# Inverse roots from one activation table, and the order of work around the first self-attention

## The reference, cut to what matters

```python
x = x + tanh(g_xattn) * xattn(layernorm(x), ctx)        # 16 heads of 128, 361 context tokens
h = layernorm(x)                                        # (x - m) / sqrt(v + 1e-5)
a = rms(h, w_ln1)                                       # x * rsqrt(mean(x^2) + 1e-6) * w
q, k, v = a @ wq + bq, a @ wk + bk, a @ wv + bv         # 16 heads of 32
q, k = rope(q, k)
h = h + softmax(causal(q @ k.T * 32**-0.5)) @ v @ wo
b = rms(h, w_ln2)
route = top_2(softmax(b @ w_router))                    # 8 experts
out = x + tanh(g_ffn) * (h + routed(b) + silu(b @ g) * (b @ u) @ d * sigmoid(b @ eg))
```

## Time and profile before

| | |
|---|---|
| median of 3 runs | 1021.59 us |
| lowest, highest run | 1018.97 us, 1024.71 us |
| the profiled execution's own time | 1021.96 us |
| its span, first to last instruction | 1020.2 us |
| mean granted clock of PE | 0.956 of full speed |
| busy: PE, DVE, ACT, POOL | 900.8, 659.8, 588.1, 391.8 us |
| table loads on ACT | 27, of 1283 ns each |

### The profile page before, as it was taken

The page is one execution under the profiler, slowest core; times in us unless marked ns, Lnnn a source line. Parts: engine busy times, 40 slices in busy tenths (PEclk is TensorE's granted clock), DMA queues, the critical chain, the costliest instruction groups (busy, mean ns, idle before and its releaser), DMA issues.

```text
span 1020.2 us, 16174 instructions
## 1 busy us (share of the span) xinstructions
PE 900.8 (88%) x5713; PEld 829.2 (81%) x5713; DVE 659.8 (65%) x1504; ACT 588.1 (58%) x1455; POOL 391.8 (38%) x367
## 2 busy tenths in 40 slices
PE   5999999999999999989775888898985898988896
PEld 4889999999989999989644866787984887877785
DVE  3557777734657777747565765674655778786653
ACT  3656766644556666634488325675443667776751
POOL 3432222346522222347211732342045365565531
PEclk9999999999999999999775998899998899999998
DMA  5762000045500000054111221132267699999875
GB/s 142 210 227 76 1 1 1 11 128 147 162 27 16 1 1 2 12 146 128 32 46 31 74 70 52 52 94 78 88 221 204 199 301 278 305 280 289 273 189 142
DMA packets 125689, 120.76 MB, mean 118 GB/s; under 512 B 12645, under 2 KB 96557, under 8 KB 125009
## 3 DMA queue, kind: packets, MB, share of 16 engines
q1 hardware_dynamic: 106510, 96.09, 30.8%
q0 software_dynamic: 5120, 10.22, 4.9%
q10 hardware_dynamic: 13978, 13.41, 4.6%
HBM read 102.16 MB, written 17.53 MB: 117 GB/s over the span
## 4 chain that ended last, share of the span: by engine, by line
PE 50%; DMA 17%; DVE 12%; ACT 10%; issue 5%; POOL 4%; SPq 0%; ACTq 0%; POOLq 0%; DVEq 0%
PE bank L1968 45%; DMA eraw<-in_L_ffn_w_down_e_dram 5%; DMA eraw<-in_L_ffn_w_up_e_dram 4%; PE bank L2095 3%; DMA s_sum<-yo,target 3%; ACT PF L1087 2%; DVE we L1313 2%; ACT we L878 2%; POOL s_rows L1901 1%; DMA s_rows<-HR,idx 1%; ACT wf L864 1%; DMA sums<-s_sum 1%; POOL wx L1832 1%; DMA raw<-in_L_xattn_Wo_dram 1%; ACT L1087 1%
## 5 line engine op out<-in xcount | busy, mean ns | idle before, releaser
L1861 POOL TENSOR_SCALAR SC<-SC,mx,anyv 100x361 f32<-100x361 f32 x128 | 81.5, 647 | 211.0 <-DVE mx L1426 200.8
L1844 POOL TENSOR_TENSOR we<-eraw,we 128x704 fp32r<-128x704 f32 x40 | 70.7, 1768 | 138.1 <-ACT we L878 137.8
L878 ACT ACTIVATE we<-eraw 128x704 fp32r<-128x704 f32 (+2 forms) x140 | 97.0, 719 | 45.9 <-DMA eraw<-in_L_ffn_w_up_e_dram 20.9
L1313 DVE TENSOR_TENSOR we<-eraw,we 128x704 fp32r<-128x704 f32 (+2 forms) x100 | 94.1, 956 | 44.9 <-ACT we L878 44.8
L1832 POOL TENSOR_TENSOR wx<-raw,wx 128x512 fp32r<-128x512 f32 x64 | 84.0, 1320 | 93.6 <-ACT wx L864 93.5
L1832 POOL TENSOR_TENSOR wf<-raw,wf 128x512 fp32r<-128x512 f32 x48 | 63.6, 1328 | 137.2 <-ACT wf L864 137.2
L1968 PE MATMUL bank<-H2h,wf 128*128 128x400 f32 x352 | 105.2, 363 | 9.4 <-DVE wf L1313 6.6
L993 ACT ACTIVATE SC<-SC,mx 100x361 f32<-100x361 f32 x128 | 75.4, 593 | 27.8 <-DVE mx L1422 27.2
L1968 PEld LDWEIGHTS bank<-H2h,wf 128*128 128x128 f32 x352 | 68.5, 197 | 12.7 <-DVE wf L1313 8.4
L1968 PE MATMUL bank<-XTh,wx 128*128 128x400 f32 x256 | 72.6, 357 | 3.2 <-POOL wx L1832 1.9
L1968 PE MATMUL bank<-QOh,wx 128*128 128x400 f32 x256 | 73.8, 357 | 0.0
(11 more groups left out here) (266 smaller groups left out, 2787.1 us busy)
## 6 DMA issues: line engine op xcount, KB each, us to landing
eraw<-in_L_ffn_w_gate_e_dram SPq DMA_DIRECT2D x40, 352.0 KB, 4.1
eraw<-in_L_ffn_w_up_e_dram SPq DMA_DIRECT2D x40, 352.0 KB, 5.4
eraw<-in_L_ffn_w_down_e_dram SPq DMA_DIRECT2D x40, 256.0 KB, 6.1
raw<-in_L_xattn_Wq_dram SPq DMA_DIRECT2D x32, 256.0 KB, 3.1
raw<-in_L_xattn_Wo_dram SPq DMA_DIRECT2D x32, 256.0 KB, 3.0
raw<-in_L_ffn_w_sh_gate_dram SPq DMA_DIRECT2D x22, 256.0 KB, 2.9
raw<-in_L_ffn_w_sh_up_dram SPq DMA_DIRECT2D x22, 256.0 KB, 3.4
s_rows<-Z SPq DMA_DIRECT2D x6, 800.0 KB
```

The costliest lines, as they stand in the source:

```text
L878: eng.activation(weights("e", u)[0:rows, 0, 0:n], eraw[u % 6][0:rows, 0:n], ACT.Copy).then_inc(sem("act_e"), 1)
L1313: return eng.tensor_tensor(o, src, f32(hi), ALU.subtract)
L1844: eng.tensor_tensor(w[0:rows, 1, 0:n], eraw[u % 6][0:rows, 0:n], f32(w[0:rows, 0, 0:n]), ALU.subtract).then_inc(sem("pool_e"), 1)
L1861: eng.tensor_scalar(sc, sc, m[:, 3, h:h + 1], anyv[:, b:b + 1], ALU.mult, ALU.mult).then_inc(sem("pool_p"), 1)
```

## The change

Each inverse root becomes two activations, exp(-0.5 * ln(var + eps)), in a helper `inverse_root`, and the reciprocals on DVE go away. Ln and Exp are both in the table `natural_log_exp_and_others`, which is loaded by hand in three places: as ACT's first instruction, after the Tanh of the two gates, and ahead of the last four roots. The compiler still adds loads for Tanh and Silu. In all 7 loads are left of 27.

The order changes too. All eight `qk(1, n)` now stand beside steps 12 to 19 of the first self-attention (five stood beside steps 15 to 19, and three behind it). The norm work of the second half begins at step 2 instead of step 5 and goes on to step 12 instead of 15. Three of the four `wo` groups that stood beside steps 0 to 3 move ahead of the self-attention. At the end of the second half, three shared-expert groups move from behind the norm to between the `po(1, m)`.

```diff
+ROOT_TABLE = "natural_log_exp_and_others"
@@ steps_ffn
-        if n in (5, 7):
+        if n in (3, 5, 7):
             yield from take(wo, 1)
     yield ("rope", 0, 7)
-
-    beside = {0: take(wo, 1), 1: take(wo, 1), 2: take(wo, 1), 3: take(wo, 1), 4: [("vbat", 0, 0), fetch],
...
+    yield from take(wo, 2)
+
+    beside = {0: take(wo, 1), 1: [("vbat", 0, 0), fetch], 2: [("vadd", 0, 0), ("resid", 4)],
...
+              10: [("turn", 6), ("square", 7), ("ffn_constants",)], 11: [("row", 7)], 12: [("turn", 7), fetch, ("qk", 1, 0)]}
+    beside |= {12 + n: [fetch, ("qk", 1, n), ("rope", 1, n - 1)] for n in range(1, 8)}
     for n in range(4 * HB + 4):
         yield ("at", 0, n)
         yield from beside[n]
-    for n in range(5, 8):
-        yield from (fetch, ("qk", 1, n), ("rope", 1, n - 1))
+    yield ("router_split",)
...
     for m in range(KD):
         yield from (fetch, ("po", 1, m))
+        if m < 3:
+            yield from take(s0, 1)
...
-    for n in (1, 1, 1, 1, 1, 1, 2, 1, 1, 1):
+    for n in (1, 1, 1, 1, 1, 1, 1, 1, 0, 0):
         yield from take(ep, 1)
         yield from take(s0, n)
@@ scalar_program
+        def inverse_root(o, var, eps):
+
+            own[0] += 1
+            eng.activation(o, var, ACT.Ln, bias=eps).then_inc(sem("act_own"), 1)
+            act.wait_ge(sem("act_own"), own[0])
+            return eng.activation(o, o, ACT.Exp, scale=-0.5)
@@ tanh_gates
+            eng.preload_act_table_set(ROOT_TABLE)
@@ norm1, and likewise x_root, square, eroot
-            eng.activation(rs[:, b:b + 1], mv[:, b, 1:2], ACT.Sqrt, bias=eps1[:, 0:1]).then_inc(sem("act_root1"), 1)
+            inverse_root(rs[:, b:b + 1], mv[:, b, 1:2], eps1[:, 0:1]).then_inc(sem("act_root1"), 1)
@@ eroot
+            if b == HB:
+                eng.preload_act_table_set(ROOT_TABLE)
@@ vector_program, norm1, and likewise x_norm, row, erms
-            chained(eng.reciprocal(rs[:, b:b + 1], rs[:, b:b + 1]))
```

More of the change, by code:

```diff
@@ L244, in steps_ffn @@
             yield ("rope", 0, n - 1)
-        if n in (5, 7):
+        if n in (3, 5, 7):
             yield from take(wo, 1)
     yield ("rope", 0, 7)
-    beside = {0: take(wo, 1), 1: take(wo, 1), 2: take(wo, 1), 3: take(wo, 1), 4: [("vbat", 0, 0), fetch],
-              5: [("vadd", 0, 0), ("resid", 4)], 6: [("vbat", 0, 1), fetch, ("norm1", 4), ("ffn_constants",)],
-              7: [("vadd", 0, 1), ("resid", 5), ("square", 4)], 8: [("vbat", 0, 2), ("row", 4), ("norm1", 5)],
-              9: [("vadd", 0, 2), ("turn", 4), ("resid", 6), ("square", 5)], 10: [("vbat", 0, 3), ("row", 5), ("norm1", 6)],
-              11: [("vadd", 0, 3), fetch, fetch, ("turn", 5), ("resid", 7), ("square", 6)], 12: [("row", 6), ("norm1", 7)],
-              13: [("turn", 6), ("square", 7)], 14: [("row", 7)], 15: [("turn", 7), fetch, ("qk", 1, 0)],
-              16: [fetch, ("qk", 1, 1), ("rope", 1, 0)], 17: [fetch, ("qk", 1, 2), ("rope", 1, 1)],
-              18: [fetch, ("qk", 1, 3), ("rope", 1, 2)], 19: [fetch, ("qk", 1, 4), ("rope", 1, 3), ("router_split",)]}
+    yield from take(wo, 2)
+    beside = {0: take(wo, 1), 1: [("vbat", 0, 0), fetch], 2: [("vadd", 0, 0), ("resid", 4)],
+              3: [("vbat", 0, 1), fetch, ("norm1", 4)], 4: [("vadd", 0, 1), ("resid", 5), ("square", 4)],
+              5: [("vbat", 0, 2), ("row", 4), ("norm1", 5)], 6: [("vadd", 0, 2), ("turn", 4), ("resid", 6), ("square", 5)],
+              7: [("vbat", 0, 3), ("row", 5), ("norm1", 6)],
+              8: [("vadd", 0, 3), fetch, fetch, ("turn", 5), ("resid", 7), ("square", 6)], 9: [("row", 6), ("norm1", 7)],
+              10: [("turn", 6), ("square", 7), ("ffn_constants",)], 11: [("row", 7)], 12: [("turn", 7), fetch, ("qk", 1, 0)]}
+    beside |= {12 + n: [fetch, ("qk", 1, n), ("rope", 1, n - 1)] for n in range(1, 8)}
     for n in range(4 * HB + 4):
@@ L851, in scalar_program @@
         fetched = {"x": 0, "f": 0, "e": 0}
+        own = [0]
+        def inverse_root(o, var, eps):
[3 more added lines that the diff above has]
+            return eng.activation(o, o, ACT.Exp, scale=-0.5)
         def fetch(stream):
@@ L894, in x_root @@
             act.wait_ge(sem("pool_const"), CONST["eps"])
-            eng.activation(rs[:, b:b + 1], mv[:, b, 1:2], ACT.Sqrt, bias=eps1[:, 0:1]).then_inc(sem("act_root"), 1)
+            inverse_root(rs[:, b:b + 1], mv[:, b, 1:2], eps1[:, 0:1]).then_inc(sem("act_root"), 1)
         def x_turn(half, i):
@@ L1038, in square @@
             act.wait_ge(sem("dve_ms1"), b + 1)
-            eng.activation(rz[:, b:b + 1], ms[:, b:b + 1], ACT.Sqrt, bias=eps2[:, 0:1]).then_inc(sem("act_rz"), 1)
+            inverse_root(rz[:, b:b + 1], ms[:, b:b + 1], eps2[:, 0:1]).then_inc(sem("act_rz"), 1)
         def turn(b):
@@ L1100, in eroot @@
             b = h * HB + i
+            if b == HB:
+                eng.preload_act_table_set(ROOT_TABLE)
             act.wait_ge(sem("dve_ms2"), b + 1)
-            eng.activation(rz[:, b:b + 1], ms[:, b:b + 1], ACT.Sqrt, bias=eps2[:, 0:1]).then_inc(sem("act_rz2"), 1)
+            inverse_root(rz[:, b:b + 1], ms[:, b:b + 1], eps2[:, 0:1]).then_inc(sem("act_rz2"), 1)
         def eh(h, i):
@@ L1481, in row @@
             dve.wait_ge(sem("dve_z"), b + 1)
-            chained(eng.reciprocal(rz[:, b:b + 1], rz[:, b:b + 1]))
             stt(HR[b % 3][:, 0:D], Z[:, b, :], rz[:, b:b + 1], ln1b[:, :], ALU.mult, ALU.mult).then_inc(sem("dve_row"), 1)
```

## The result

The changed kernel takes 1013.97 us (median of 8 runs, 1010.23 to 1018.95), the kernel before, measured beside it, 1021.85 us (8 runs, 1018.97 to 1024.71). The ratio is 0.9928, with a 95% interval of 0.9903 to 0.9953. So it is faster by 0.7%, 7.9 us, where 20 us were forecast, and the time lies 0.03 us inside the upper end of the forecast range (991 to 1014 us). The profiled execution took 1013.93 us, with a span of 1012.1 us.

The account below looks back on a forecast made before the run. Waits between engines, with ACT's table loads, bound the first self-attention. Gains 1.6 + 8.3 + 15.8 - 2.8 = 22.9 us, less 2.7 for clock, leave 20; 1021.96 - 20 + 0.2 + 0.5 = 1002.7, forecast 1002.5 us, range 991 to 1014.

Parts of the forecast that it names:

- What bound the kernel: First self-attention to the norm behind it: no engine full, waits between engines set the time; sixteen loads of 1.28 us.
- Roots: Inverse roots: Ln 0.29 and Exp 0.19 us, 0.48 against 0.45 us per norm; 0.2 us added for eight roots.
- Ahead of the steps, and steps 0 to 4: POOL's extra subtraction at qk(0, 3) costs 0.5 us; step 4's exponentials at 504.7 instead of 506.3, 1.6 us gained.
- Steps 4 to 12: First self-attention, steps 4 to 11: DVE sets the pace, 29.6 us instead of 37.9, 8.3 us gained.
- the prediction's own sign (step 12 late): First self-attention: if step 12 itself comes late (expected near 534 us), DVE was not the only limit.
- The 5 us for the clock: Scores and first qk tile: PE's low granted clock costs 5 us in all; half taken, as 2.7 us.
- From step 12 to the first rotation: First self-attention: turn(7) in step 12, qk(1, 0) right behind; 5.5 us instead of 21.3, 15.8 us gained.
- The rotations: First rotation to po(0, 1): three minima, normalisations and two copies add 2.8 us on DVE, the limit there.
- Rival B: First self-attention stage: engines wait in turn, DVE stays at 66 to 70%; 1009 to 1014.5 us, chance 0.22.
- Rival E: Steps 12 to 19: PQ waits for rotations, exponentials queue behind; slower from 6.7 us a step on, chance 0.02.
- The rest: Behind po(1, m): two loads gone -2.6 us, load before router's Tanh +1.3, moved groups; 0 taken together, 3 either way.
- rival A: The forecast itself: DVE sets the pace, rotations begin some 25 us earlier; 995 to 1009 us, chance 0.60.

Follow-up runs that it names:

- tables_only: The changed kernel's new inverse roots, with the step order of the kernel before; 1014.35 us, ratio 0.9918 to the kernel before.
- order_only: The changed kernel's step order, with Sqrt, reciprocals and their loads as in the kernel before; 1022.72 us, ratio 1.0017 to the kernel before.
- rope_first: The changed kernel with rotation rope(1, n-1) ahead of fetch and qk(1, n) beside steps 13 to 19; 1011.87 us, ratio 0.9891 to the kernel before.
- qk_later: The changed kernel with the first qk(1, n) tile beside step 12, the next five beside 15 to 19, two behind; 1010.29 us, ratio 0.9898.
- wo_behind: The changed kernel with the wo group of n = 3 moved behind rope(0, 7); 1016.35 us in one run.
- qk_at_14: The changed kernel with the qk(1, n) tiles beside steps 14 to 19, two behind, and the rotation ahead of fetch and tile; 1007.22 us, ratio 0.9872.
- ring_dve: The changed kernel with three weight subtractions, of the fetches beside steps 13 to 15, on DVE instead of POOL; 1013.90 us, ratio 0.9932.
- best: The changed kernel with rotation first, tiles one step later, Exp/Tanh table loaded behind the last root, one shared-expert group ahead of the picks; 1005.58 us, ratio 0.9850.
- shared_back: The changed kernel with the three shared-expert groups back behind po(1, m); 1014.00 us, ratio 0.9924 to the kernel before.
- router_load: The changed kernel with the table of Exp and Tanh loaded behind the last root; 1012.39 us, ratio 0.9899 to the kernel before.
- plain_at_13: The changed kernel with each qk(1, n) tile one step later, the first beside step 13, order inside a step kept; 1008.06 us, ratio 0.9872.

## Why the prediction was half right

**What bound the kernel: right.** The loads on ACT set the pace of the steps (ACT 20.12 of 20.62 us busy between steps 8 and 12), and taking them away is the whole gain (tables_only and order_only). The price of a load was right too, 1.28 us. The Trainium skill's page "ScalarE: Activation LUTs", section "What ACT_TABLE_LOAD costs", puts a switch at about 2.66 us; eight switches stood between steps 8 and 12, 21.3 us by that page (an estimate), more than the whole 20.62 us. The trace does not agree: beside 10.3 us of loads ACT did 9.9 us of other work there, and the drain isn't seen.

**Roots: right.** Ln is 0.30 us, Exp 0.20 us. The load at the start does not delay ACT's transfers (first issue at 0.79 us, 0.76 before).

**Ahead of the steps, and steps 0 to 4: mis-sized by about a microsecond.** The +0.5 us for POOL's subtraction did not come: the last sum ends 25.3 instead of 24.0 us after the first shuffle, but the first exponentials start 27.7 us after it, 27.8 before. From the exponentials of step 0 to those of step 4 it was 12.6 us (493.77 to 506.32) and is 12.0: 0.5 us gained, not 1.6. The mark itself is later (508.59), since the stage ahead of it began later. Its first rotation starts at 468.83, at 465.93 before; but in the 11 other kernels that are the same up to there it starts between 465.15 (rope_first) and 468.38 us (qk_later). So most of that belongs to the one execution.

**Steps 4 to 12: the pace was right at first, the size wrong.** 8.3 us were forecast, 4.7 came. In steps 4 to 8 DVE is busy 13.70 of 15.50 us, the fullest engine, as said. In steps 8 to 12 it is 11.48 of 17.71 us, at a granted clock of 0.61, and the engines wait in turn. By the prediction's own sign (step 12 late) DVE was not the only limit. The 5 us for the clock, of which I took half (2.7 is a slip for 2.5), stood over the whole stage. These are steps 4 to 8 in two kernels with the same instructions there and the same DVE work, first wo_behind, then qk_at_14:

```profile
504.89:522.99 18.10, 13.61 (x116) 9.96 (x116) 13.79 (x31) 8.87 (x45) 0.00 (x0) 0.81 0.12 36
```

```profile
507.00:522.51 15.51, 12.42 (x116) 9.01 (x116) 13.70 (x31) 9.00 (x45) 0.00 (x0) 0.89 0.15 42
```

Of the 12 kernels with this order in steps 4 to 8, three took 15.5 us at a granted clock of 0.89 (the changed one, qk_at_14, qk_later), two 17.1 at 0.90 (ring_dve, best) and seven 18.0 to 18.3 at 0.81. So a lower clock goes with the longest ones, but it is not all of it. The profiled run of the changed kernel is one of the shorter ones here, by luck; at about 18.1 us E is 93.5 to 93.8, as in wo_behind, shared_back and router_load, and steps 4 to 12 gain only 2 us.

**From step 12 to the first rotation: the mechanism was right.** 15.8 us were forecast, 14.1 came (21.3 down to 7.2). The first tile took 3.8 us (544.36 to 548.18), with a granted clock of 0.51 from 544.36 to 547.40, the lower level of 1.2 GHz, and 1.00, that is 2.4 GHz, at 548. What I left out is that the exponentials of step 13 stand behind it.

**The rotations: the step that failed.** The prediction took three minima, normalisations and copies as 2.8 us more, on a DVE that never waits. It is 9.0 us (34.8 against 25.9), and 7.9 of them are DVE's waits for POOL's cosine (10.9 against 3.0); DVE's own work grew by 1.0 only. So the term that failed is the wait that the prediction put at nothing. The cause is a ring of waits of 5.6 us per step, through the weight copy, the subtraction and the cosine. rope_first takes the waits down to 1.0 us and the rotations to 30.9 us; there the stretching of DVE's instructions, for which I had set up to 5 us into the range, does come (28.1 instead of 23.4 us). ring_dve shows that the place of the subtraction, not POOL, makes the ring. The other cause is the late step 13, which pushes softmax steps among the rotations: with step 13 ahead of the tile (plain_at_13) they take 31.6 us. I had looked at each engine's sum of work and not at what stands ahead of what on POOL. Rival B names this kind of wait, and its time, 1009 to 1014.5 us, is the one that came. DVE is busy 59.5 of the 91.2 us of E, 65%, near B's 66 to 70%, where 75% or more were forecast. But its chain (`PF`, `PQ`, tile, normalisation) lacks the link that mattered. Rival E had a ring through `PQ` that decides from 6.7 us a step on; the one that came takes 5.6 us.

**The rest: I took 0, with 3 us either way.** X is 2.9 us longer than before, a third of the 8.6 us that E gained. order_only has X 91.3 us with the same order and Sqrt, so it comes with the tables. Against order_only, counted from the first `YTf`, the router's Exp comes 0.4 us later (39.0 and 38.5), the Tanh and the picks 1.8 us (picks 45.0 and 43.1), the first write of a row by POOL 2.3 us (64.4 and 62.1) and the first transfer 3.4 us. So the +1.3 us of the load at Tanh was right, on its row (2.33 against 0.92 us) and on the path to the picks; router_load did not refute it, since it put the load elsewhere on that path. What adds the last 1.6 us behind the picks is open. The 2.6 us for the two loads came on the way to the last root, but not to the rows: counted from the last of the four `YTf` copies, that root starts after 16.9 us before, 14.2 in order_only and 14.9 in the changed kernel, while X of order_only is only 0.5 us shorter than before.

**The number.** The sum of the steps, 22.9 us, was 10.3 (0.5 + 4.7 + 14.1 - 9.0). That the time fell inside the range at all is luck: it is 11.5 us from the forecast, outside the range of rival A and inside that of B.
